# GpSimd in place of VectorE for the column scaling of W_conv in a graph-network layer

## The reference, cut to what matters

```python
h = maximum(layernorm(x), 0)
xn = batchnorm(h, norm1_g, norm1_b)
agg = segment_sum(xn[src], dst, 1250) / maximum(deg, 1)[:, None]   # 20000 edges
conv_out = relu(agg @ W_conv + b_conv)
# attention: one graph, its first 256 rows, 8 heads of 64, 256 random features (proj)
attn = performer(h[:256] @ Wq, h[:256] @ Wk, h[:256] @ Wv, proj) @ Wo
out = x + batchnorm(conv_out + attn_at(pos) + h, norm2_g, norm2_b)
```

## Time and profile before

| | |
|---|---|
| median of 3 runs | 180.65 us (180.29 to 180.94) |
| profiled execution: its own time | 180.8 us |
| profiled execution: its span | 178.8 us |
| TensorE busy | 162.6 us, 91% |
| VectorE busy | 136.9 us, 77% |
| ScalarE busy | 90.6 us, 51% |
| GpSimd busy | 7.6 us, 4% |

### The profile page before, as it was taken

The page is one execution under the profiler, slowest core; times in us unless marked ns, Lnnn a source line. Parts: engine busy times, 40 slices in busy tenths (PEclk is TensorE's granted clock), DMA queues, the critical chain, the costliest instruction groups (busy, mean ns, idle before and its releaser), DMA issues.

```text
span 178.8 us, 2873 instructions
## 1 busy us (share of the span) xinstructions
PE 162.6 (91%) x1060; PEld 106.7 (60%) x1061; DVE 136.9 (77%) x309; ACT 90.6 (51%) x164; POOL 7.6 (4%) x22
## 2 busy tenths in 40 slices
PE   0299999998999999999999999999999999999950
PEld 0288888653445464664777779585465484664840
DVE  2888659979685859699774885994999998596681
ACT  3437959567796639996643444324900313104050
POOL 5008200000000000000000000000000000000000
PEclk9999999999999999999999999999999999999998
DMA  5996970000070000000000000000096005040036
GB/s 180 370 307 213 315 236 4 0 0 0 6 252 0 0 4 0 0 0 2 4 0 4 0 0 4 0 0 7 9 312 251 0 4 143 2 133 14 0 101 187
DMA packets 11883, 13.69 MB, mean 77 GB/s; under 512 B 1458, under 2 KB 6748, under 8 KB 11868
## 3 DMA queue, kind: packets, MB, share of 16 engines
q1 hardware_dynamic: 10476, 12.13, 21.2%
q10 hardware_dynamic: 1072, 1.10, 1.8%
q0 software_dynamic: 320, 0.26, 0.6%
HBM read 10.92 MB, written 2.56 MB: 75 GB/s over the span
## 4 chain that ended last, share of the span: by engine, by line
PE 79%; DVE 11%; ACT 4%; DMA 2%; issue 2%; DVEq 0%; ACTq 0%
PE bank L959 23%; PE bank L695 19%; PE bank L625 10%; PE bank L719 4%; PE bank L709 4%; PE bank L738 4%; PE bank L637 3%; PE bank L617 3%; PE bank L683 2%; DMA xs<-in_x 2%; PE bank L672 2%; PE bank L986 2%; DVE wc L1122 1%; DVE mxk L1145 1%; DVE xs L1387 1%
## 5 line engine op out<-in xcount | busy, mean ns | idle before, releaser
L695 PE MATMUL bank<-wc,xs 128*128 128x512 f32 (+1 forms) x80 | 38.5, 608 | 0.2 <-DVE gl L1198 0.2
L959 PE MATMUL bank<-r,gl 128*128 128x512 f16 (+1 forms) x120 | 38.1, 338 | 0.0
L959 PE MATMUL bank<-r,gh 128*128 128x512 f16 (+1 forms) x120 | 38.1, 339 | 0.0
L1066 DVE TENSOR_TENSOR ohb<-iota,bcol 128x1280 f16<-128x1280 f16 x25 | 20.4, 818 | 3.8 <-PE bank L637 3.7
L385 ACT ACTIVATE r<-bank 128x500 f16<-128x500 f32 x25 | 18.6, 770 | 3.4 <-PE bank L637 3.4
L695 PEld LDWEIGHTS bank<-wc,xs 128*128 128x128 f32 (+1 forms) x80 | 13.6, 187 | 10.9 <-issue 10.9
L625 PE MATMUL bank<-hT,r 128*128 128x256 f32 x64 | 17.6, 439 | 0.0
L959 PEld LDWEIGHTS bank<-r,gh 128*128 128x128 f16 x120 | 11.6, 97 | 9.7 <-issue 0.3
L959 PEld LDWEIGHTS bank<-r,gl 128*128 128x128 f16 x120 | 11.7, 97 | 9.3
L595 ACT ACTIVATE bw<-mv,epst 128x1 f32<-128x1 f32 x4 | 1.2, 295 | 31.4 <-DVE mv L1363 31.4
L625 PEld LDWEIGHTS bank<-hT,r 128*128 128x128 f32 x64 | 14.0, 223 | 2.9 <-issue 0.4
(11 more groups left out here) (175 smaller groups left out, 263.5 us busy)
## 6 DMA issues: line engine op xcount, KB each, us to landing
xs<-in_x SPq DMA_DIRECT2D x15, 256.0 KB, 4.8
out<-xs SPq DMA_DIRECT2D x7, 256.0 KB
r<-in_L_gnn_Wq SPq DMA_DIRECT2D x1, 1024.0 KB, 7.5
r<-in_L_gnn_Wk SPq DMA_DIRECT2D x1, 1024.0 KB
wc<-in_L_gnn_W_conv SPq DMA_DIRECT2D x1, 1024.0 KB, 9.4
wvo<-in_L_gnn_Wv SPq DMA_DIRECT2D x1, 1024.0 KB, 12.0
wvo<-in_L_gnn_Wo SPq DMA_DIRECT2D x1, 1024.0 KB, 5.2
xs<-in_x ACTq DMA_DIRECT2D x3, 256.0 KB, 4.4
```

Source lines behind the costliest of these rows:

```text
L695: last = nc.tensor.matmul(acc[0:n, :], xnT[:, f, i * P:i * P + n], wc[:, f, :], start=(f == 0), stop=(f == FT - 1))
L959: last = nc.tensor.matmul(acc[:, 0:cn], gg[0:n, s, f * P:(f + 1) * P], A16[0:n, s, c0:c0 + cn], start=(s == 0 and gg is gh), stop=(s == NT ...
L1066: last = V.tensor_tensor(oh[:, s0:s0 + n, :].rearrange("p s (m t) -> p s m t", t=2), iota16[:, 0:size].rearrange("p (m t) -> p m t", t=2). ...
```

## The change

The four multiplications of `wc` by `crow` leave VectorE's order and are put at the end of GpSimd's, behind a wait for `crow_ready`. The wait of VectorE for its own `crow_ready` goes too. All else is as it was.

```diff
@@ block.gpsimd, after the indirect DMAs
+            pool.wait_ge(crow_ready, 1)
+            for f in range(FT):
+                nc.gpsimd.tensor_tensor(wc[:, f, :], wc[:, f, :], crow[:, :], ALU.mult).then_inc(wc_scaled, 1)
@@ block.vector, column_scales
                 V.tensor_scalar(crow_i[:, :], crow_i[:, :], -1.0, float(SCALE_BITS), ALU.mult, ALU.add).then_inc(crow_ready, 1)
-                dve.wait_ge(crow_ready, 1)
-
-            def scale_weights(f):
-                V.tensor_tensor(wc[:, f, :], wc[:, f, :], crow[:, :], ALU.mult).then_inc(wc_scaled, 1)
@@ block.vector, the order
             bn_scale()
             diagonals(0)
-            for f in range(FT):
-                scale_weights(f)
             one_hots()
             key_max(0)
```

## The result

The changed kernel takes 182.2 us (median of 5 runs, 181.77 to 183.22), the kernel before 180.85 us, likewise of 5 (the 180.65 above is the median of the first three). The ratio is 1.0103 with a 95% interval of 1.0072 to 1.0133: about 1% slower, by 1.4 us between the medians. Forecast were 181.5 us and slower by 0.65 to 0.85 us. The side was right, and so was the mechanism, a hold of VectorE by GpSimd; the size was too small.

The account below looks back on a forecast made before the run. TensorE, busy 91% of the span, was taken to bound the kernel. VectorE's 2.8 us delay from holds, less 1.95 us won by removal, gave 0.85 us slower: median about 181.5 us, range 179.5 to 182.6.

Parts of the forecast that it names:

- Where TensorE waits, and what removal alone is worth: TensorE idles only behind VectorE's order between 38 and 50 us; removing the four multiplications alone gains 1.0 us.
- Both gaps: TensorE's waits of 0.73 us before the count of group 1 and 0.27 us before the features at 48.17.
- The hold: A VectorE operation meeting a running GpSimd operation waits for its end, then both take turns; inferred from one cast row.
- The price T of a multiplication: One 128x512 fp32 multiplication on GpSimd takes 1.07 us, from the affine select's slope.
- d = 4T - 1.5: Delay of ScalarE's release by four holds less idle time and overlap, 2.8 us; time moves by d - 1.95, never below -1.0.
- The cover of GpSimd itself: GpSimd's products end by 39.6 or 43.5 us, before TensorE could want them at 48.5; cover 2.3 times its slowest time.
- The turns: GpSimd goes first from 35.3 us, alternating with VectorE's ohb and ohv of group 0, then bn_scale's small operations; L1134 ends at 41.74.
- The cover of 1.03 us: Of about 4.3 us of holds, 1.03 us fall where VectorE would have idled anyway.
- The forecast of 0.85: key_max(3) ends at 45.86 instead of 45.01, so TensorE's features start 0.85 us later and the kernel loses that in full.
- No hold: Rival: both engines run beside each other, both TensorE gaps close, 179.65 us; chance 0.30.
- Shorter or fewer holds: Rival: GpSimd quicker or only two or three operations held, 180.1 to 181.2 us; chance 0.22.
- The multiplication of 2.04 us: Rival: GpSimd's multiplication at its upper bound with full holds, 4.7 us slower, 185.4 us; chance 0.06.

Follow-up runs that it names:

- e1_none: Kernel before without the four wc multiplications and TensorE's wait for them, so wc is unscaled: 179.59 us against 180.43, ratio 0.9959.
- e3_later: Changed kernel with GpSimd's multiplications also waiting for VectorE's one-hots of group 1: 178.98 us against 180.43 for the kernel before, ratio 0.9916.
- e8_vector_later: Kernel before with VectorE's four multiplications moved behind q_bias(1) and the one-hots of group 2, GpSimd doing nothing: 179.3 us against 180.59, ratio 0.9939.
- e10_later_again: Changed kernel with GpSimd waiting for the one-hots of group 1, measured a second time: 178.97 us against 180.25 for the kernel before, ratio 0.9922.
- e6_long: Kernel before plus fourteen GpSimd multiplications of 128x512 fp32 into spare tiles behind crow_ready: 192.2 us in one execution.
- e5_fills: Kernel before plus ten GpSimd fills of 128x512 fp32 into spare tiles behind crow_ready: 180.62 us against 180.59, ratio 0.9989.
- e11_after_bn: Changed kernel with GpSimd also waiting for bn1_ready, so it starts behind bn_scale: 180.05 us against 180.16 for the kernel before, ratio 1.000.
- e12_again: Changed kernel unaltered, measured a third time: 182.29 us against 180.16 for the kernel before, ratio 1.0128.
- e4_again: Changed kernel unaltered, measured a second time: 182.51 us against 180.43 for the kernel before, ratio 1.0139.
- e2_spare_work: Kernel before, VectorE's multiplications kept, plus four GpSimd multiplications into unread spare tiles behind crow_ready: 184.03 us against 180.43, ratio 1.0213.
- e9_scales_first: Changed kernel with column_scales put ahead of bn_mean on VectorE: 182.27 us against 180.25 for the kernel before, ratio 1.0103.
- e7_half: Kernel before with wc tiles 0 and 1 multiplied on GpSimd, 2 and 3 left on VectorE: 180.82 us against 180.59, ratio 1.0029.

## Why the prediction was right or wrong

**Where TensorE waits, and what removal alone is worth: right.** Both gaps closed in the four profiles where the work is gone from its old place and nothing holds bn_scale or the one-hots (e1_none, e3_later, e8_vector_later, e10_later_again); the stretch from the count of group 0 to the first product with wc fell from 10.82 us to between 9.69 and 9.72. The forecast was 1.0, the profiles show 1.1. That the times of e3_later, e8_vector_later and e10_later_again fell by 1.3 to 1.5 us, and e1_none, which does less, by 0.8, the profiles don't explain: the stretch is equal in them. It stays open.

**The hold: right, but the row that it was built on doesn't show it.** Spare multiplications that nobody reads cost 3.6 us, fills nothing. The one row, a cast of two elements 0.09 us longer than another, is of an operation with one input, and e6_long held none of the three kinds with one input that it met (the reciprocal kept 0.18 us, the reduction 0.67). The cast takes 0.25 to 0.26 us in all fourteen profiles, always beside the same select and issued 0.09 us before the cast ahead of it ends, so nothing tells what lengthens it. Nor does a one-input row bear out the Trainium skill's rule on two inputs (SBUF — State Buffer, section Who interferes with whom), as I had said; the rows of the experiments do. That the inference from it came true is luck in this respect. That only two-input operations are held I did not know from the rows; here it changed little, since nearly all of bn_scale has two.

**The price T of a multiplication: too small.** I took 1.07 us from the slope of the affine select. Measured were 1.22 to 1.23 us from one hold's end to the next, 1.26 recorded. By my own rule, d = 4T - 1.5 and a loss of d - 1.95, T = 1.22 gives 1.4 us in place of 0.85. That this is close to the 1.35 us measured between the medians is chance, as the next paragraph shows: in the sequence on VectorE the longer T was made up for. The Trainium skill's figure (GPSIMD Engine Reference, section Elementwise side-by-side cycle accounting), by which I had put an estimate of 1.17 us beside the sum, was nearer than mine. The cover of GpSimd itself was misreckoned: from 35.3 to 48.5 us are 13.2 us, 1.6 times the slowest time of 8.2 us and not 2.3 times; nothing hung on it, since the last product ended at 42.3 us.

**The turns: wrong, and by luck without consequence.** GpSimd did not come first. VectorE had both one-hots through, neither was stretched, and all four holds fell on bn_scale, not two; only the reciprocal ran beside GpSimd without one. In the rows of before, ohb waited for ScalarE's columns until 0.25 us after crow was done; where VectorE runs later against ScalarE it doesn't, and ohb is issued as crow ends (36.35 and 36.37 us), before GpSimd sees crow at 36.45. But my sequence had 41.74 - 35.43 = 6.31 us from the issue of ohb to the end of L1134, and the three profiles of the changed kernel show 6.34, 6.34 and 6.36. Two errors cancelled: in the first profile the holds took 4.70 us (37.60 to 42.30) where I had 4.15, and what VectorE did outside them took 1.64 where I had 2.16.

**The cover of 1.03 us: the step that failed.** "1.03 us of them VectorE would have idled anyway" took the idle time of one execution as given. In the three profiles of the changed kernel VectorE's idle time before the reciprocal was nothing, nothing and 0.66 us. It hangs on the play between VectorE's chain and TensorE's, the time from the issue of ohb to TensorE's count of group 0:

| profile | play, us | idle before the reciprocal, us |
|---|---|---|
| before | 3.25 | 1.03 |
| e3_later | 3.32 | 1.10 |
| e5_fills | 3.06 | 0.84 |
| e8_vector_later | 3.02 | 0.80 |
| e10_later_again | 2.46 | 0.25 |
| e1_none | 2.39 | 0.18 |
| e11_after_bn | 2.39 | 0.17 |
| changed kernel, e12_again | 2.88 | 0.66 |
| changed kernel, e4_again | 2.26 | none |
| changed kernel, first profile | 2.13 | none |

The idle time is the play less 2.2, and I had planned with nearly the best of them. Before the change, the idle time takes up the play and TensorE notices nothing. With four holds on bn_scale, what is missing of the play is a later release of ScalarE, and TensorE waits for the difference. The forecast of 0.85, plus what is missing to 3.25, gives 1.97 us for the first profile, 1.84 for e4_again and 1.22 for e12_again; from the count of group 0 to the features at 48.17 (9.49 us before) they took 2.21, 2.08 and 1.48 us longer. The last 0.24 to 0.26 us come mostly from features("uk", 2): its start moved 0.15 us by the wait for ScalarE's copies (46.33 - 44.29 against 44.85 - 42.96).

Where the play comes from can be followed on VectorE's side. Its chain starts at the landing of the indirect DMAs, and from there to ohb it is 9.40 to 9.41 us in all six profiles without the wait for crow_ready in which ohb doesn't wait for ScalarE, and 9.52 to 9.54 in the six with it (the removed wait is worth 0.13 us, which I had put at nothing). In the first profile of the changed kernel the DMA landed 1.3 us later than in the profile of before:

```profile
25.68 0.29 DVE L1080 TENSOR_SCALAR r<-r 125x256 int32<-125x256 int32 x1 [1.93 <-DMA r<-in_dst,rows]
```

```profile
26.94 0.29 DVE L1084 TENSOR_SCALAR r<-r 125x256 int32<-125x256 int32 x1 [2.33 <-DMA r<-in_dst,rows]
```

In e4_again it landed as before (25.64), and TensorE was at the count of group 0 1.4 us sooner (37.31 against 38.68). So both ends of the play move from one execution to the next. That the loss between the medians (1.35 us) is made up in the same way is argued from these three profiles; the play of the executions without a profile isn't known.

**The clock.** Not in the forecast at all. A longer gap can bring a stretch at a lower granted clock, as in e2_spare_work. That it belongs to the changed kernel's slower executions is likely by the clocks above, and not shown in a profile of it.

**The chances.** No hold had 0.30: it is excluded here. Shorter or fewer holds, 0.22: excluded with all four tiles on GpSimd, though the half version behaves so. The multiplication of 2.04 us, 0.06: it took 1.22.

## What to carry to other kernels

Moving elementwise work from VectorE to GpSimd isn't free of VectorE even when GpSimd is idle: each GpSimd operation that reads SBUF can hold a two-input operation on VectorE for its whole length, so look at what VectorE does in the very microseconds in which GpSimd would run, and let it run beside reductions and copies. A chain of tiny dependent operations is no safer than a larger operation: each link of 0.16 us paid up to 1.03 us, about as much as ohv of 0.40 us did in e9_scales_first (1.07), and as many links paid as GpSimd had multiplications. Before paying another engine for it, see whether the work can stand later in VectorE's own order (here 0.6% for nothing), and never count an idle time of one execution as cover without asking what it gives way to.

## What the runs showed of the hardware

- GpSimd's fp32 multiplication of 128x512 takes 1.22 to 1.26 us with two different inputs. With the same tile as both inputs the holds of e2_spare_work were 0.96 us long and 0.99 to 1.00 apart (the first was shorter); its output was a tile of its own too, so which of the two shortens it isn't shown.
- A GpSimd multiplication issued 0.1 us after ohb waited for ohb and for the ohv behind it (2.15 us recorded), while in e9_scales_first, where GpSimd had come first, the two engines took strict turns. In the records of e7_half GpSimd starts 0.02 us before ohb and still waits (2.29 us recorded), in e11_after_bn 0.03 us before ohb and holds it (1.92 us). What decides where the two come so close together wasn't tried.
- TensorE's granted clock fell to a mean of 0.65 for 4.1 us behind a gap of 3.54 us, and stayed at 1.00 behind one of 2.26 us (changed kernel, first profile, 44 to 52 us).
